# Second attention: scores as two-part float32r products of head pairs in the two row halves of the array, and a full-array bfloat16 matmul ahead of each unit of exponentials

## The chip, the cores and the metric

The kernel runs on one core of one Trainium2 chip. The metric is the device time in microseconds of one execution; three runs of the kernel before stand below. Engines: PE (TensorE matmul), PEld (its weight loads), DVE (VectorE), ACT (ScalarE), POOL (GpSimd), SP (the queue that issues DMAs).

## The reference, cut to what matters

The network is attention A, a two-layer feed-forward stage, attention B, the same feed-forward stage again, each with a residual. Only attention B is changed: 4 sequences of 1024 tokens, 16 heads of 8 dimensions, causal softmax.

```python
Q = split_heads(einsum('bsd,od->bso', x, Wq)); K, V likewise   # x: layer norm of the input
Q = _apply_rope(Q, cos, sin);  K = _apply_rope(K, cos, sin)
logits = jnp.einsum('bhnd,bhmd->bhnm', Q, K) / sqrt(8)
logits = jnp.where(causal, logits, -jnp.inf)
probs = jax.nn.softmax(logits, axis=-1)
attn = jnp.einsum('bhnm,bhmd->bhnd', probs, V)
x = x + einsum('bsd,od->bso', attn, Wo)
```

## The kernel before, in words

Attention B (`attn_b_stage`) works on 16 groups of 4 heads. Queries and keys after the rotation are split into three bfloat16 parts (`first_part`, `second_part`, `third_part`; buffer `RP`, stored to DRAM by `store_parts`). `load(m)` brings a group back so that the nine products of parts times 8 dimensions lie in 72 rows of `QS` and `KS`; three more rows hold the negated row maximum of the scores, so 75 rows are contracted.

Every score is computed twice. A **maximum unit** (`max_unit`, L1661) writes scores of 128 queries against up to 512 keys into one of two one-bank buffers `s1`, on the diagonal after a mask matmul (L1658); DVE reduces the bank to its maximum (L1965). After a group's maxima, POOL splits the 32 negated maxima of each partition into three parts (`offsets`), PE turns them (`turn_unit`, L1670), DVE copies them to `MT` (L1982), and `rows` sends them by one DMA (L1541) into the last three rows of `QS`. An **exponential unit** (`exp_unit`, L1693) writes scores of 128 keys against up to 1024 queries of one head (or several heads of short rows) into one of two two-bank buffers `s2`; ACT writes the exponentials to `PT` (L1876), which holds two key tiles. For groups 3 to 15 POOL zeroes the future part of the diagonal tile (L2089); for groups 0 to 2 a mask matmul (L1688) does it. A **value block** (`value_block`, L1711) multiplies four heads' exponentials with the values, four 128x32 f32 matmuls side by side in the array's columns, into one of two banks `o` (queries 0 to 511, and 512 to 1023); column sums come out with it. ACT copies `o` out (L1865), SP sends it back to rows of heads.

`step(n)` writes the PE order by hand. It runs over 8 slots: in slot j the exponential units of group n for key tile j, the value blocks of tile j-1, and between them the maximum units of group n+1 (slots 0 to 3 of 8) or n+2 (slots 4 to 7), query tiles in the order `MAX_TILES`. A step has 22 exponential units, 12 value blocks of 512, 384, 256 or 128 columns (6, 2, 2, 2 of them), 38 maximum units and 22 mask matmuls. DVE, ACT and POOL follow the same order; each engine works in order, and waits are on counts.

## Time and profile before

| | us |
|---|---|
| median of 3 runs (lowest, highest) | 2239.9 (2236.67, 2242.97) |
| the profiled execution, its own time | 2241.25 |
| its span, first to last instruction | 2239.5 |
| PE busy in the span | 2057.4 (92%) |
| DVE busy | 1786.7 (80%) |
| ACT busy | 1387.7 (62%) |
| POOL busy | 1233.0 (55%) |

The busy shares are averages over stages with different limits. Attention B runs from about 891 us to 1500 us of the span; its first score is written at 928.5 us. The copies of the turned maxima (one in each step) mark the steps. A busy time of PE includes modelled ends of matmuls, so the distance between two starts, not the duration in a row, tells what a matmul cost the array.

### The profile page before, as it was taken

What the parts mean: (1) busy time and instruction counts of PE and PEld (TensorE: products, weight loads), DVE (VectorE), ACT (ScalarE), POOL (GpSimd) and SP (SyncE); (2) the same over time, 40 slices, a digit from 0 to 9 for tenths busy, and PEclk for the clock granted to TensorE, in tenths of its full rate; (3) what the DMA queues carried; (4) which work ended last, traced back from release to release, by engine and by line L of the source; (5) the groups of instructions that cost most, each with busy time, mean ns of one, the idle gap of its engine ahead of it and who ended that gap; (6) DMA issues with size and microseconds to landing.
All of it is one profiled execution on the core that took longest, in us unless ns stands there. A gap on an engine that the chain in (4) does not pass through costs nothing. (4 is left out here: it accounts for less than half of the span.)

```text
span 2239.5 us, 44709 instructions
## 1 busy us (share of the span) xinstructions
PE 2057.4 (92%) x16567; PEld 1066.7 (48%) x16567; DVE 1786.7 (80%) x2386; ACT 1387.7 (62%) x3475; POOL 1233.0 (55%) x633
## 2 busy tenths in 40 slices
PE   5677899999999997899999999968899999999997
PEld 2224555555555553443333333314555555555554
DVE  6986889899999993666777777707899899899993
ACT  8455566666666664446666665665666666766663
POOL 0117777777777771235121222127877777777770
PEclk9799999999999999889999999998999999999999
DMA  2004112112111111303111111122111111111111
GB/s 62 0 3 125 35 34 49 34 36 47 35 43 40 34 34 30 119 29 100 48 44 52 54 40 43 31 61 81 31 44 39 36 43 42 34 44 39 35 34 43
DMA packets 86075, 101.14 MB, mean 45 GB/s; under 512 B 13817, under 2 KB 59841, under 8 KB 83557
## 3 DMA queue, kind: packets, MB, share of 16 engines
q1 hardware_dynamic: 83429, 96.58, 16.8%
q8 instruction: 135, 2.21, 0.4%
q10 hardware_dynamic: 2432, 1.70, 0.3%
q14 instruction: 79, 0.65, 0.1%
HBM read 35.98 MB, written 8.39 MB: 20 GB/s over the span
## 5 line engine op out<-in xcount | busy, mean ns | idle before, releaser
L840 POOL TENSOR_TENSOR ffn_RN<-ffn_SS,ffn_mhalf 128x16 f32<-128x16 f32 x128 | 372.5, 2910 | 272.7 <-DVE ffn_SS L786 272.2
L1965 DVE TENSOR_REDUCE attn_b_NX<-attn_b_s 128x1 f32<-128x512 f32 (+3 forms) x608 | 381.4, 660 | 131.7 <-PE attn_b_s L1661 126.4
L834 POOL TENSOR_TENSOR ffn_QK<-ffn_T 128x1024 f32<-128x1024 f32 x128 | 421.3, 3292 | 20.2 <-DVE ffn_T L734 20.0
L581 ACT ACTIVATE ffn_PB<-ffn_s,ffn_NM 128x128 f32<-128x128 f32 x1024 | 360.6, 391 | 102.6 <-DVE ffn_NM L756 102.6
L1876 ACT ACTIVATE attn_b_PT<-attn_b_s 128x1024 f32<-128x1024 f32 (+3 forms) x352 | 298.1, 870 | 192.3 <-PE attn_b_s L1693 187.9
L625 ACT ACTIVATE ffn_SQ<-ffn_w 128x1024 f32<-128x1024 f32 x128 | 131.1, 1024 | 311.4 <-DVE ffn_T L734 311.1
L828 POOL TENSOR_TENSOR ffn_PB<-ffn_PB,ffn_RDEN 128x1024 f32<-128x1024 f32 x128 | 243.7, 1904 | 27.1 <-DVE ffn_RDEN L719 27.1
L370 PE MATMUL ffn_w<-ffn_Wqkv,ffn_H 128*128 128x512 f32 x512 | 245.9, 603 | 10.5 <-ACT ffn_SQ L625 4.7
L581 ACT ACTIVATION_READ_ACCUMULATOR ffn_PB<-ffn_s,ffn_NM 128x1 f32 x1024 | 236.9, 231 | 0.0
L1661 PE MATMUL attn_b_s<-attn_b_KS,attn_b_QS 72*128 72x512 bf16 (+3 forms) x768 | 220.7, 336 | 6.2 <-DVE attn_b_NX L1965 5.5
L750 DVE TENSOR_TENSOR ffn_QK<-ffn_QK,ffn_RN 128x1024 f32<-128x1024 f32 x128 | 218.7, 1709 | 0.4 <-POOL ffn_RN L840 0.3
L773 DVE COPY ffn_PT<-ffn_w 128x1024 f32<-128x1024 f32 x128 | 156.2, 1221 | 69.3 <-PE ffn_w L424 68.9
L2089 POOL TENSOR_SCALAR_AFFINE_SELECT attn_b_PT<-attn_b_PT 128x512 f32<-128x512 f32 x104 | 66.8, 642 | 252.5 <-ACT attn_b_PT L1876 251.2
L445 PE MATMUL ffn_m<-ffn_HN,ffn_W 128*114 128x512 f32 x360 | 185.9, 613 | 9.0 <-ACT ffn_G L609 3.2
L1693 PE MATMUL attn_b_s<-attn_b_QS,attn_b_KS 75*128 75x512 bf16 (+3 forms) x768 | 187.0, 333 | 5.9 <-ACT attn_b_PT L1876 4.3
L731 DVE TENSOR_TENSOR ffn_T<-ffn_w,ffn_rope 128x1024 f32<-128x1024 f32 x128 | 154.9, 1210 | 40.4 <-PE ffn_w L370 40.2
L1711 PE MATMUL attn_b_o<-attn_b_PT,attn_b_VQ 128*32 128x512 f32 (+3 forms) x1536 | 166.2, 505 | 3.6 <-POOL attn_b_PT L2089 3.3
L756 DVE TENSOR_REDUCE ffn_NM<-ffn_s 128x8 f32<-128x1024 f32 x128 | 155.7, 1217 | 13.5 <-PE ffn_s L412 13.5
L734 DVE TENSOR_TENSOR ffn_T<-ffn_w,ffn_rope 128x512 f32<-128x512 f32 x256 | 163.7, 681 | 0.0
L783 DVE TENSOR_REDUCE ffn_SS<-ffn_SQ 128x16 f32<-128x1024 f32 x128 | 154.6, 1208 | 2.2 <-ACT ffn_SQ L625 2.2
L424 PEld LDWEIGHTS ffn_w<-ident,ffn_PB 128*128 128x128 f32 x1024 | 117.9, 143 | 77.7 <-issue 59.9
L370 PEld LDWEIGHTS ffn_w<-ffn_Wqkv,ffn_H 128*128 128x128 f32 x512 | 95.0, 193 | 119.5 <-issue 82.3
(257 smaller groups left out, 3765.9 us busy)
## 6 DMA issues: line engine op xcount, KB each, us to landing
ffn_Voff<-ffn_Vcur SPq DMA_DIRECT2D x248, 128.0 KB, 2.3
attn_b_QS<-attn_b_qk_parts SPq DMA_DIRECT2D x48, 192.0 KB
attn_b_KS<-attn_b_qk_parts SPq DMA_DIRECT2D x48, 192.0 KB
ffn_H<-ffn_Y SPq DMA_DIRECT2D x64, 128.0 KB, 2.5
ffn_H<-ffn_U SPq DMA_DIRECT2D x64, 128.0 KB, 2.5
attn_b_qk_parts<-attn_b_RP SPq DMA_DIRECT2D x6, 768.0 KB, 4.4
ffn_rope<-in_ffn_rope_dram SPq DMA_DIRECT2D x4, 1024.0 KB, 7.9
attn_b_rope<-attn_b_OS SPq DMA_DIRECT2D x252, 16.0 KB
```

Source lines behind the costliest of these rows:

```text
L370: last = pe.matmul(w0_ps[:, c, :], H1[:, g % 2, b, :], Wqkv[:, l, c, :], start=True, stop=True)
L445: pe.matmul(mlp_bank(g, half, j), W1[:, g // NT, half, j, :], HN[:, :], start=True, stop=True)\
L581: last = act.activation(PB[:, x % 2, e, p, :], s_ps[:, e, p * P:(p + 1) * P], ACT.Exp, bias=NM[:, x % 2, e, p:p + 1], accum_out=DEN[:, x % ...
L750: dve.tensor_tensor(qk, qk, RN[:, x % 2, :].unsqueeze(2).broadcast_to([P, 2 * NH, DH]), ALU.mult)\
L828: pool.tensor_tensor(probs_x, probs_x, by, ALU.mult).then_inc(normed, 1)
L834: pool.tensor_tensor(QK[:, x % 2, :, :, :].rearrange("p c q k -> p (c q k)"), T1[:, :, :, :].rearrange("p c h k -> p (c h k)"), T2[:, :, : ...
L840: pool.tensor_tensor(RN[:, x % 2, :], SS[:, x % 2, :], mhalf[:, :], ALU.pow).then_inc(rnorm, 1)
L1661: last = pe.matmul(bank[:, q * width:(q + 1) * width], QS[0:KS9, m % RING, g + q, i * P:(i + 1) * P], KS[0:KS9, m % RING, g + q, lo:hi], s ...
L1693: last = pe.matmul(bank[:, q * pitch + lo:q * pitch + hi], KS[:, n % RING, g + q, j * P:(j + 1) * P], QS[:, n % RING, g + q, j * P + lo:j ...
L1711: last = pe.matmul(o_ps[half][VCOLS * g:VCOLS * (g + 1), lo - half * 512:512], VQ[:, n % 2, g, j, :], PT[:, j % 2, g, lo - j * P:hi - j * ...
L1876: act.activation(PT[:, j % 2, g:g + pack, 0:width], s2_ps[k % 2][:, 0:pack * pitch].rearrange("p (q w) -> p q w", q=pack)[:, :, 0:width], ...
L1965: dve.tensor_reduce(NX[:, m % 2, c, g:g + pack, i], s1_ps[k % 2][:, 0:pack * (hi - lo)].rearrange("p (q w) -> p q w", q=pack), AX_X, ALU.m ...
```

## The change

All of it is in attention B.

- **Parts.** Rotated queries and keys are split into two float32r parts instead of three bfloat16 ones: one ACT copy (rounded to float32r) and one subtraction for each, instead of two copies and two subtractions. Four products of parts times 8 dimensions take 32 rows.
- **Pairs.** Heads of a group lie in the two halves of the partitions: rows 0 to 63 (`par` 0) and 64 to 127 (`par` 1). Each matmul of scores contracts 62 or 64 rows, some of them zeros (32 terms, zeros, and two rows for the offsets). The zeros and ones are written once by four POOL memsets.
- **Exponential units** hold a pair of heads: 512 queries at most of `par` 0 in one bank of `s2`, of `par` 1 in the other. A step goes over 12 pieces (query half, key tile), with 20 such units. Ahead of the scores of a unit stands a full-array bfloat16 matmul of the identity with the mask table, as many columns as the unit has in a bank, into the bank that the scores then overwrite. In groups 0 to 2 the units on the diagonal have four 64-row mask matmuls instead.
- **Maximum units**: 38 as before, each of one `par`; three banks `s1` instead of two. A mask is two matmuls over 64 rows and 64 columns of keys.
- **Value blocks** stay 12 of the same shapes, but both halves go into one bank `o`; they lag the exponentials by two pieces, and `PT` is a ring of four pieces.
- The offsets take two POOL operations instead of four, the offset rows four DMAs instead of one, a load eight DMAs instead of six.
- `step` spreads the maximum units by columns: behind each exponential unit as many as keep up with the columns of the exponentials.

```diff
-PARTS = 3
-KS9 = PARTS * PARTS * BD
+PARTS = 2
+TERMS = PARTS * PARTS * BD
+NPAR, NPR = 2, 2
+HROWS = P // NPAR
+OFFSETS = HROWS - PARTS
+PIECES_OF = [(0, j) for j in range(4)] + [(1, j) for j in range(8)]
+PRING, PLAG = 4, 2
+S1_BANKS = 3
...
-        s1_ps = [ps(f"s1_{i}", [P, 512]) for i in range(2)]
-        o_ps = [ps(f"o_{i}", [P, 512]) for i in range(2)]
+        s1_ps = [ps(f"s1_{i}", [P, 512]) for i in range(S1_BANKS)]
+        o_ps = ps("o", [P, 512])
...
-                sp.dma_start(QS[KS9:KS9 + PARTS, m % RING, :, :].rearrange("a g t -> a (g t)"), MT[:, m % 2, :])\
-                  .then_inc(s_rows[m % 2], 16)
+                for par in range(NPAR):
+                    for a in range(PARTS):
+                        at = par * HROWS + OFFSETS + a
+                        of = (a * NPAR + par) * NPR * NT
+                        sp.dma_start(QS[at:at + 1, m % RING, :, :].rearrange("a q t -> a (q t)").bitcast(F32),
+                                     MT[of:of + NPR * NT, m % 2, :]).then_inc(s_rows[m % 2], 16)
...
             def max_unit(...):
-                wait(pe, s1_read, k - 1)
+                wait(pe, s1_read, k + 1 - S1_BANKS)
...
-                    last = pe.matmul(bank[:, q * width:(q + 1) * width], QS[0:KS9, m % RING, g + q, i * P:(i + 1) * P],
-                                     KS[0:KS9, m % RING, g + q, lo:hi], start=not diagonal, stop=True,
+                rows = rows_for(par, OFFSETS)
+                for q, (i, c, pr) in enumerate(segments):
+                    last = pe.matmul(bank[:, q * width:(q + 1) * width], QS[rows, m % RING, pr, i * P:(i + 1) * P],
+                                     KS[rows, m % RING, pr, c * 512:c * 512 + width], start=not diagonal, stop=True,
...
+            def exp_unit(n, s, u):
+                bank = [s2_ps[k % 2][:, par * 512:par * 512 + pack * w] for par in range(NPAR)]
+                masked = n < SELECTS and diagonal(s)
+                if masked:
+                    for h in range(2):
+                        for par in range(NPAR):
+                            at = bank[par].rearrange("p (q w) -> p q w", q=pack)[:, :, h * HROWS:(h + 1) * HROWS]
+                            mask(at, par, 1, h, pack, h == 0)
+                else:
+                    pe.matmul(bank[0], keep["identb"][:, :],
+                              causal[:, :, :, :].rearrange("p a b c -> p (a b c)")[:, 0:pack * w], start=True, stop=True,
+                              skip_group_check=True)
                 for q in range(pack):
+                    for par in range(NPAR):
+                        rows = rows_for(par, HROWS)
+                        last = pe.matmul(bank[par][:, q * w:(q + 1) * w],
+                                         KS[rows, n % RING, first + q, j * P:(j + 1) * P],
+                                         QS[rows, n % RING, first + q, lo:hi], start=not masked and q == 0, stop=True,
...
+            def value_block(n, s):
                 if j == 0:
-                    wait(pe, o_read[half], n)
+                    wait(pe, o_read[1 - half], n + half)
...
             def step(n, first):
+                for s in range(NPIECE if 0 <= n < NG else 0):
+                    at = n * NPIECE + s - PLAG
+                    if at >= 0:
+                        value_block(*divmod(at, NPIECE))
+                    for u in range(len(exp_units(s))):
+                        exp_unit(n, s, u)
+                        exps += exp_columns(s, u)
+                        while done < len(scores) and columns * ALL_EXPS < exps * ALL_SCORES:
+                            slot, v = scores[done]
+                            ...
+                                max_unit(m, slot, v)
```

The order on **PE**, in the middle of a step. Before (`s1` maximum units with scores of `KS`, `s2` exponential units, `o` a value block; the last number of a buffer's name is its bank):

```order
L1693 MATMUL attn_b_s2_0<-attn_b_QS,attn_b_KS 128x512
L1693 MATMUL attn_b_s2_0<-attn_b_QS,attn_b_KS 128x384
L1661 MATMUL attn_b_s1_0<-attn_b_KS,attn_b_QS 128x512
L1693 MATMUL attn_b_s2_1<-attn_b_QS,attn_b_KS 128x512
L1693 MATMUL attn_b_s2_1<-attn_b_QS,attn_b_KS 128x384
L1661 MATMUL attn_b_s1_1<-attn_b_KS,attn_b_QS 128x512
L1711 MATMUL attn_b_o_0<-attn_b_PT,attn_b_VQ 32x512 x4
L1661 MATMUL attn_b_s1_0<-attn_b_KS,attn_b_QS 128x512
L1661 MATMUL attn_b_s1_1<-attn_b_KS,attn_b_QS 128x512
L1693 MATMUL attn_b_s2_0<-attn_b_QS,attn_b_KS 128x512
```

PE at the same place of a step, now (L1728 is the added full-array matmul, L1734 the pair of scores for the exponentials, L1677 a mask half, L1696 the scores for a maximum):

```order
L1728 MATMUL attn_b_s2_0<-attn_b_causal,identb 128x512
L1734 MATMUL attn_b_s2_0<-attn_b_QS,attn_b_KS 128x512 x2
L1677 MATMUL attn_b_s1_0<-attn_b_causal 128x64 x2
L1696 MATMUL attn_b_s1_0<-attn_b_KS,attn_b_QS 128x384
L1696 MATMUL attn_b_s1_1<-attn_b_KS,attn_b_QS 128x512
L1728 MATMUL attn_b_s2_1<-attn_b_causal,identb 128x512
L1734 MATMUL attn_b_s2_1<-attn_b_QS,attn_b_KS 128x512 x2
L1696 MATMUL attn_b_s1_2<-attn_b_KS,attn_b_QS 128x512
L1696 MATMUL attn_b_s1_0<-attn_b_KS,attn_b_QS 128x512
L1753 MATMUL attn_b_o<-attn_b_PT,attn_b_VQ 32x512 x4
```

The full-array matmul now stands between 64-row matmuls on either side, and the maximum units come two at a time behind an exponential unit.

The order on **ACT** around the copy of the first query half (`attn_b_OS`) in a step. Before:

```order
L1876 ACTIVATE attn_b_PT<-attn_b_s2_1 128x640
L1876 ACTIVATE attn_b_PT<-attn_b_s2_0 128x2x512
L1876 ACTIVATE attn_b_PT<-attn_b_s2_1 128x2x512
L1876 ACTIVATE attn_b_PT<-attn_b_s2_0 128x2x384
L1865 ACTIVATE attn_b_OS<-attn_b_o_0 128x512
L1876 ACTIVATE attn_b_PT<-attn_b_s2_1 128x2x384
```

ACT there now:

```order
L1925 ACTIVATE attn_b_PT<-attn_b_s2_0 128x1024
L1909 ACTIVATE attn_b_OS<-attn_b_o 128x512
L1925 ACTIVATE attn_b_PT<-attn_b_s2_1 128x1024
L1925 ACTIVATE attn_b_PT<-attn_b_s2_0 128x1024
L1925 ACTIVATE attn_b_PT<-attn_b_s2_1 128x1024
```

The copy reads the bank that the next value block of the other half starts; before, the other half had a bank of its own.

The order on **SP** in one step (results back to rows of heads, offset rows from `MT`, loads of a later group). Before:

```order
L1532 DMA attn_b_rope<-attn_b_OS 8x512 x4
L1536 DMA attn_b_rope<-attn_b_OS 8x512 x4
L1541 DMA attn_b_QS<-attn_b_MT 3x32x128
L1532 DMA attn_b_rope<-attn_b_OS 8x512 x4
L1536 DMA attn_b_rope<-attn_b_OS 8x512 x4
L1514 DMA attn_b_QS<-attn_b_qk_parts 24x1x4096 x3
L1520 DMA attn_b_KS<-attn_b_qk_parts 24x1x4096 x3
```

SP in one step now:

```order
L1553 DMA attn_b_rope<-attn_b_OS 8x512 x4
L1557 DMA attn_b_rope<-attn_b_OS 8x512 x4
L1566 DMA attn_b_QS<-attn_b_MT 1x16x128 x4
L1553 DMA attn_b_rope<-attn_b_OS 8x512 x4
L1557 DMA attn_b_rope<-attn_b_OS 8x512 x4
L1540 DMA attn_b_QS<-attn_b_qk_parts 16x1x2048 x4
L1540 DMA attn_b_KS<-attn_b_qk_parts 16x1x2048 x4
```

The places are the same; the offset rows are four DMAs in a row, the load eight.

## Rows read from the trace of the kernel before

**Rows 1.** Busy time by stretch: us, engines busy (count), PE clock, DMA share, GB/s

```profile
972.90:1008.60 35.70, 34.77 (x199) 13.44 (x199) 24.64 (x42) 18.27 (x22) 8.28 (x8) 0.76 0.01 2
...
1363.40:1394.80 31.40, 30.04 (x217) 10.83 (x215) 24.11 (x42) 19.49 (x26) 6.46 (x13) 1.00 0.17 48
...
1457.70:1488.60 30.90, 25.30 (x186) 6.65 (x184) 0.27 (x1) 23.04 (x30) 7.23 (x12) 0.94 0.07 14
```

**Rows 2.** Instructions on tile `attn_b_s`: duration ns min/median/max, first and last start us

```profile
L1982 DVE CAST attn_b_MT<-attn_b_s x16: 274/276/288, 972.9 to 1457.7; 96x128 bf16<-96x128 f32 x16
```

**Rows 3.** Waits in 1363.4 to 1394.8 us: us in total, times, longest us

```profile
ACT attn_b_PT L1876 <- PE attn_b_s L1693: 12.6, 14, 1.6
PEld attn_b_s L1658 <- DVE attn_b_NX L1965: 7.7, 15, 0.8
DVE attn_b_NX L1965 <- PE attn_b_s L1661: 7.0, 13, 0.8
```

**Rows 4.** Timeline of PE inside steps: start us, duration us, instructions

```profile
1249.81 0.38 PE L1661 MATMUL attn_b_s<-attn_b_KS,attn_b_QS 72*128 72x512 bf16 x1
1250.12 1.06 PE L1711 MATMUL attn_b_o<-attn_b_PT,attn_b_VQ 128*32 128x512 f32 x8
1251.11 0.23 PE L1658 MATMUL attn_b_s<-attn_b_causal,identb 128*128 128x128 bf16 x1
...
1251.40 0.22 PE L1658 MATMUL attn_b_s<-attn_b_causal,identb 128*128 128x128 bf16 x1
1251.46 0.38 PE L1661 MATMUL attn_b_s<-attn_b_KS,attn_b_QS 72*128 72x512 bf16 x1
1251.68 0.49 PE L1693 MATMUL attn_b_s<-attn_b_QS,attn_b_KS 75*128 75x512 bf16 x2
...
1372.23 0.43 PE L1711 MATMUL attn_b_o<-attn_b_PT,attn_b_VQ 128*32 128x128 f32 x8
1372.59 0.39 PE L1658 MATMUL attn_b_s<-attn_b_causal,identb 128*128 128x512 bf16 x1
```

**Rows 5.** Timeline of PE in the second feed-forward stage, at its 64x64 tiles

```profile
1703.57 0.59 PE L379 MATMUL ffn_w<-ffn_Wqkv,ffn_H 128*128 128x512 f32 x1
1704.09 0.41 PE L403 MATMUL ffn_s<-ffn_masks,identb 64*64 64x512 bf16 x4
1704.33 1.04 PE L412 MATMUL ffn_s<-ffn_KT,ffn_QT 64*64 64x128 f32 x32
1705.30 1.11 PE L445 MATMUL ffn_m<-ffn_HN,ffn_W 128*114 128x512 f32 x2
```

**Rows 6.** Groups by form, 1363.4 to 1394.8 us: busy us, mean ns | idle before, releasers

```profile
L1965 DVE TENSOR_REDUCE attn_b_NX<-attn_b_s 128x1 f32<-128x512 f32 x24 | 15.6, 687 | 3.1 <-PE attn_b_s L1661 3.0
...
L1876 ACT ACTIVATE attn_b_PT<-attn_b_s 128x1024 f32<-128x1024 f32 x7 | 6.8, 1027 | 4.3 <-PE attn_b_s L1693 4.3
...
L1865 ACT ACTIVATE attn_b_OS<-attn_b_o 128x512 f32<-128x512 f32 x3 | 1.8, 592 | 0.0
```

**Rows 7.** Busy time by stretch (columns as in rows 1), at the lower clock

```profile
976.40:983.10 6.70, 6.70 (x23) 2.92 (x23) 3.53 (x6) 3.56 (x4) 1.16 (x1) 0.50 0.01 2
...
928.50:938.70 10.20, 9.15 (x39) 7.58 (x40) 2.67 (x4) 3.08 (x4) 4.36 (x3) 0.50 0.48 151
```

**Rows 8.** The offset rows of the first group, and what PE does next (timeline)

```profile
973.24 0.81 SPq L1541 DMA_DIRECT2D attn_b_QS<-attn_b_MT  x1
...
977.35 1.06 PE L1693 MATMUL attn_b_s<-attn_b_QS,attn_b_KS 75*128 75x512 bf16 x2
```

**Rows 9.** The third parts on DVE (timeline), and a memset on POOL (group by form)

```profile
912.45 2.43 DVE L1942 TENSOR_TENSOR attn_b_RP<-attn_b_TA,attn_b_RP 128x1024 bf16<-128x1024 f32 x2
...
L2024 POOL MEMSET attn_b_VQ<- 128x2048 f32 x1 | 1.8, 1804 | 0.0
```

**Rows 10.** Last step, without maximum units: its first scores and last copy (timeline)

```profile
1462.19 1.04 PE L1693 MATMUL attn_b_s<-attn_b_QS,attn_b_KS 75*128 75x512 bf16 x4
...
1487.94 0.60 ACT L1865 ACTIVATE attn_b_OS<-attn_b_o 128x512 f32<-128x512 f32 x1 [1.33 <-PE attn_b_o L1711]
```

More of the change, by code:

```diff
@@ new lines, in turn_unit @@
+                pe.wait_ge(parts, PARTS * (m + 1))
+                pe.matmul(s1_ps[k % S1_BANKS][0:PARTS * BG * NT, 0:P],
+                          NP[:, m % 2, :, :, :, :].rearrange("p a g h i -> p (a g h i)").bitcast(F32),
+                          keep["ident"][:, :], start=True, stop=True).then_inc(s1_mm, 1)
+            def exp_unit(n, s, u):
+                k = s2_at[n, s, u]
+                half, j = PIECES_OF[s]
+                first, pack = exp_units(s)[u]
+                lo, hi = piece(s)
+                w = hi - lo
@@ L1690, in exp_unit @@
-                for q in range(pack):
-                    for lo in range(0, width, 512):
-                        hi = min(width, lo + 512)
-                        last = pe.matmul(bank[:, q * pitch + lo:q * pitch + hi],
-                                         KS[:, n % RING, g + q, j * P:(j + 1) * P],
-                                         QS[:, n % RING, g + q, j * P + lo:j * P + hi],
-                                         start=(q * pitch + lo) % 512 == 0 if selected else lo > 0, stop=True,
+                if (s, u) == (0, 0):
+                    pe.wait_ge(s_rows[n % 2], 16 * ROWS * (n // 2 + 1))
@@ new lines, in begin_maxima, with score_columns, exp_columns @@
+            def begin_maxima(m, slot, u):
+                if u == 0 and slot == MAX_SPLIT:
+                    if m == 0:
+                        pe.wait_ge(s_set, SETS)
+                    pe.wait_ge(s_load[m % RING], 16 * LOADS * (m // RING + 1))
+            def score_columns(slot, u):
+                return max_units(slot)[u][1] * len(max_units(slot)[u][2])
+            def exp_columns(s, u):
+                return NPAR * width(s) * exp_units(s)[u][1]
+            ALL_SCORES = sum(score_columns(slot, u) for slot in range(NT) for u in range(len(max_units(slot))))
@@ L1951, in _ @@
             remainder(1)
-            for w in range(2):
-                third_part(w)
             for c in range(4, NCH):
```

489 lines of the change are left out of this document (241 added, 248 removed).

## The prediction

> **What bounds the kernel now.** I read the busy times by stretch first, then the waits of one undisturbed step, then PE's timeline inside it. Only attention B changes, so only its steps count. The copies of the turned maxima are one step apart: the first starts at 972.9, the sixteenth at 1457.7 us [rows 2], so 15 steps take 484.8 us; the step at 1363.4 is 31.4 us long with a full clock, and the first step 35.7 us with a clock of 0.76 [rows 1]. In the undisturbed step DVE is busy for 24.1 us, ACT for 19.5 [rows 1]: neither is full. PE's 30.0 us contain modelled ends, so I count its stream from start to start instead.
>
> 512 columns of bfloat16 scores take 0.22 us (1251.46 to 1251.68), 128 columns of a mask 0.06 (1251.40 to 1251.46), a value block of 512 columns 0.99 with the way out of it (1250.12 to 1251.11), one of 128 columns 0.36 (1372.23 to 1372.59), and the way into one 0.31 - 0.22 = 0.09 (1249.81 to 1250.12) [rows 4]. A group has 4 heads x 36 tiles x 128 = 18432 columns of scores, 36 times 512, and computes them twice. The stream of a step: scores 2 x 36 x 0.22 = 15.8; masks 32 x 0.06 = 1.9; value blocks 6 x 0.99 + 2 x 0.78 + 2 x 0.57 + 2 x 0.36 = 9.4 (the middle widths between the two read); ways in 12 x 0.09 = 1.1. Sum 28.2. The remaining 3.2 us of 31.4 are waits: PE's weight loads wait for DVE to free one of two banks, DVE waits 7.0 us for PE, ACT 12.6 [rows 3]. So PE bounds the step, and DVE stands 4 us behind it.
>
> **The change, part by part.** All per step of a group unless said.
>
> Value blocks keep shape and number: 9.4 + 1.1 = 10.5.
>
> Scores for the exponentials: 18 pairs of 512 columns. If two matmuls in different row halves run together, a pair costs 0.22: 18 x 0.22 = 4.0, instead of 7.9. What speaks for it: in the feed-forward stage 64x64 tiles in two row and two column halves take 32 records of 128 columns in 0.97 us (1704.33 to 1705.30); one f32 record of 512 full-array columns takes 0.52 - 0.09 = 0.43, so 32 records of 128 one after another would take 3.4 [rows 5]. Four tiles do run together. No row shows two tiles of 64 rows and 128 columns; bounds 4.0 and 7.9, I take 4.0.
>
> The type float32r is in no row. Bounds: bfloat16's 0.22 for 512 columns [rows 4], and f32, where one matmul of the program is two records of 0.43 [rows 5]. I take 0.22: the operands are rounded when they are written and split into two parts again, so they carry fewer bits than the f32 numbers that need the second record and the double passes.
> The Trainium skill (FP8 and Floating Point Precision, TensorE Precision Notes) says that true FP32 makes four passes and that a reduced-precision FP32 operand is truncated to FP22, the array's own width; by it the cost is one pass too, and no trace here shows it.
>
> Scores for the maxima with masks: 38 units as before. Alone they cost 36 x 0.22 = 7.9 and 44 mask halves x 0.06 = 2.6, in all 10.5; all in pairs half of that, 5.3. Going along PE's new order and letting only neighbours of different halves run together I count 6.3. Before: 7.9 + 1.9 = 9.8.
>
> The added full-array matmuls: as many columns as the pairs, 18 x 0.22 = 4.0. They stand between 64-row matmuls. A change of tile shape costs: 64x64 tiles follow a full-array matmul 0.52 instead of 0.43 us after its start (1703.57 to 1704.09) [rows 5], value blocks cost the 0.09 above. There are 20 such matmuls, 40 changes; 12 of the ways in come from a value block, whose way out is counted, and the turned maxima add two: 30 x 0.09 = 2.7. Bounds 0 (if full and 64-row, 128-column matmuls share a mode) and 30 x 0.14 = 4.2.
> The Trainium skill (TensorEngine Tiling, Key Properties) states that changing the tiling mode drains TensorE, which speaks against this change: by it all 30 changes cost, without it the sum would be 2.7 lower; rows 5 agree with it for the shapes they show.
>
> New stream: 10.5 + 4.0 + 6.3 + 4.0 + 2.7 + 0.3 (turn in f32) = 27.8, against 28.2. The pairs' gain of 7.4 is nearly spent on the added matmuls and their changes of shape.
>
> Waits, 3.2 before. A third bank for maxima: DVE still needs 0.69 for 512 columns [rows 6] and gets units two at a time; for a full-width piece (PE 2.65, DVE 4 x 0.69 = 2.76) I laid the units out and got 2.96, because the fourth unit must wait for a bank. Bounds: nothing, and all 3.2; I take -1.5. The single bank `o`: at two places PE's next half must wait for ACT's exponential (1.03) and the copy behind it (0.59) [rows 6], 1.8 us after the scores, while PE has 1.2 to 1.5 us of work there: 0.3 to 0.7 each, +1.0 in all; queued behind this wait are the next exponential unit and the maxima, so DVE waits too. Offset rows: one DMA issue takes 0.81 us, and PE used the rows 4.1 us after that issue began [rows 8]; three more issues make it up to 6.5, while from the turn to the step's end there are about 7. Together with weight loads of four-byte numbers, which come in twos behind each change of shape, +0.6 (bounds 0 and 3). So a step takes 27.8 + 3.2 - 1.5 + 1.0 + 0.6 = 31.1, i.e. -0.3; 15 steps -4.5.
>
> The last step has no maxima: its first scores start at 1462.2, its last copy at 1487.9 [rows 10], 26 us, bound by the chain exponential, select, value block, two pieces deep. With four pieces ACT's 20 us of exponentials and copies should bound it, or PE's 10.5 + 4.0 + 4.0 + 3.0 = 21.5, about 23: -3 (bounds -5 and 0). Start: DVE loses 2.4 us of third parts [rows 9], partly waited for elsewhere; value products now wait for ACT's copy of the single bank. -1.5 (bounds -4 and +3). The four memsets of 6144 columns take 3 times the 1.8 us of 2048 [rows 9] each, 22 us, beside the layer norm, in which POOL has nothing to do: nothing. Eight loads instead of six lie in SP's slack.
>
> Sum: 2241.25 - 4.5 - 3 - 1.5 = 2232.2 on the profiled execution's own time, which lies 1.35 above the median: 2231.
>
> **The rivals.**
> 1. *DVE becomes the bound.* PE's changes of shape fall into waits or cost less, the third bank feeds DVE without gaps. DVE's 24.1 us and a tenth for gaps and the wait at `o` make 28.5: 15 x -2.9 - 4.5: about 2192. For it: waits were equal on both sides before. Against it: PE's stream alone is 27.8.
> 2. *The row halves do not run together* (the other sign). Where: at each pair, since the second matmul's weights arrive late or the tiles exclude each other. Then scores cost 4.0 more and maxima 4.2 more, a stream of 36.0, with 1.5 of waits 37.5: 15 x 6.1 - 1.5, about 2329. If only the maxima run alone, 34.5: 2284. It decides early: my whole gain is 9 us, 0.6 a step, so with 36 pairs in a step (18 for the exponentials, 18 for the maxima) a loss of 0.02 us in each, a tenth of the 0.22, turns the sign. For it: one row above shows only 64-column tiles.
> 3. *The clock.* From 976.4 to 983.1 us PE was busy all the time with scores of 72 and 75 rows and the clock stayed at 0.50; from 928.5 it rose only after f32 value products of 128 rows [rows 7]. So it matters how much of the array works. The added full-array matmuls and the pairs speak for 2.4 GHz; lone 64-row matmuls and masks, and waits, speak against it. At 1.2 GHz the 24 us of columns double: 52 a step. All of the stage: about 2540; a third of it: about 2340.
> 4. *float32r takes more passes.* Two: +4.0 and +5, a step of 38, about 2340. Four: above 2600.
>
> **How the numbers follow.** The forecast (PE's stream swapped for one of equal length, 2205 to 2255) has 0.52, rival 1 0.18 (2180 to 2205), rival 2 0.13, rival 3 0.10, rival 4 0.07. A measurement of this kernel tells 0.3% (6.7 us) from no change. Faster than 2233.2: half of the forecast's case and rival 1, 0.45; within 0.3%: 0.16; slower: the rest of the forecast's case and rivals 2 to 4, 0.39. Both signs have weight, so the likeliest case's own range is 2205 to 2255; the range that should hold 8 times in 10 reaches from 2185, inside rival 1, to 2340, past rival 2 and the mild forms of 3 and 4.
>
> **What would show it.** Distance of the turned maxima: 31.1 here, 28.5 for rival 1, 34 and more for the others. Starts of a pair of L1734 within some ns, then 0.22 to the next: right. L1728 to L1734 0.31: the change of shape costs. Waits of L1753 for ACT's L1909 near 1 us a step. DVE near 24 us busy in 31. Clock 1.00 from the fourth step on. If the first scores of a step wait for DMA of the offset rows, my 0.6 was too small.

## The result: 1.6% slower, and the profile after

The changed kernel takes 2275.05 us (median of 4 runs, 2274.68 to 2276.26) against 2238.45 us for the kernel before (4 runs beside them): a ratio of 1.016, interval 1.0148 to 1.0172. The forecast was 2231. The profiled execution's span is 2273.1 us, 33.6 more than before. A step is the work on one group, from one copy of the turned maxima to the next; the time that a matmul holds PE is the distance from its start to the start of what follows.

The copies of the turned maxima divide these 33.6 us. First the tile's group of instructions, which answers to [rows 2], then busy times by stretch (us, engines busy (count), granted clock of PE, DMA share, GB/s), which answer to [rows 1]: first step, a late step, last step.

```profile
L2020 DVE COPY attn_b_MT<-attn_b_s x16: 273/273/282, 982.9 to 1489.1; 64x128 f32<-64x128 f32 x16
```

```profile
982.88:1013.06 30.18, 28.97 (x225) 15.48 (x226) 23.21 (x42) 17.58 (x19) 7.23 (x6) 0.83 0.01 2
...
1386.59:1420.67 34.08, 32.35 (x255) 14.88 (x258) 23.35 (x41) 19.50 (x22) 5.92 (x12) 1.00 0.17 41
1489.10:1527.70 38.60, 29.77 (x216) 10.19 (x218) 0.28 (x1) 23.35 (x29) 7.62 (x12) 0.98 0.08 14
```

- The first copy comes at 982.9 instead of 972.9 us: +9.9.
- The first three steps take 94.3 instead of 104.0 us: -9.7. The first was 35.7 us at a clock of 0.76 before [rows 1] and is 30.2 at 0.83; the third was 36.2 at 0.91 and is 32.0 at 1.00. So a good part of this gain is the granted clock and not the change.
- The other twelve take 411.9 instead of 380.7: +31.2. An ordinary one is 34.1 us where it was 31.4 [rows 1], both at a clock of 1.00; the seventh and the eleventh, which also hold the output products of a sequence, are 1.9 longer in both kernels.
- From the last copy to the end: +2.2. The last step takes 38.6 us, where before the next stage began 34.6 us after the copy: +4.0. What follows, which is not changed, was 1.8 shorter (745.4 instead of 747.2).

The profiled execution took 2274.8 us by its own time, 42.6 more than the 2232.2 forecast for it: 26.0 in the fifteen steps (+21.5 instead of -4.5), 11.4 at the start, 7.0 in the last step, less the 1.8.

The matmuls inside such a step, PE's timeline (start us, duration us, instructions), to be held against [rows 4]:

```profile
1290.58 0.39 PE L1728 MATMUL attn_b_s<-attn_b_causal,identb 128*128 128x512 bf16 x1
1290.90 0.50 PE L1734 MATMUL attn_b_s<-attn_b_QS,attn_b_KS 64*128 64x512 f32 x2
1291.24 0.40 PE L1696 MATMUL attn_b_s<-attn_b_KS,attn_b_QS 62*128 62x512 f32 x2
1291.57 0.39 PE L1728 MATMUL attn_b_s<-attn_b_causal,identb 128*128 128x512 bf16 x1
```

Two matmuls of 64 rows stand in one row (x2): the row halves run together, and 512 columns of float32r take hardly longer than 512 of bfloat16 (0.24 us from start to start in the lines below, where the forecast had 0.22), so float32r makes one pass. L1728 holds PE 0.32 us, 0.22 of columns and 0.10 of change of shape. But the pair behind it holds PE 0.34 us, not 0.22; its record is 0.50 long, that of the maxima's pair behind it 0.40. The same pairs in the run of experiment 7, which has no added matmul (L1730 is L1734 there, and the maxima are still L1696):

```profile
1330.52 0.50 PE L1730 MATMUL attn_b_s<-attn_b_QS,attn_b_KS 64*128 64x512 f32 x2
1330.85 0.40 PE L1696 MATMUL attn_b_s<-attn_b_KS,attn_b_QS 62*128 62x512 f32 x2
1331.09 0.40 PE L1730 MATMUL attn_b_s<-attn_b_QS,attn_b_KS 64*128 64x512 f32 x2
1331.33 0.93 PE L1696 MATMUL attn_b_s<-attn_b_KS,attn_b_QS 62*128 62x512 f32 x2
```

At 1330.52 the pair comes right behind a value block: 0.33 to the next. At 1331.09 it comes behind other 64-row matmuls: 0.24. So about 0.1 us hangs on what stands ahead. The weight loads (engine, count, ns min/median/max) suggest on what:

```profile
L1734 PEld LDWEIGHTS attn_b_s<-attn_b_QS,attn_b_KS x48: 182/183/186, 1388.0 to 1418.6; 64*128 64x128 f32 x48
L1696 PEld LDWEIGHTS attn_b_s<-attn_b_KS,attn_b_QS x48: 182/187/188, 1388.3 to 1420.4; 62*128 62x128 f32 x48
...
L1728 PEld LDWEIGHTS attn_b_s<-attn_b_causal,identb x20: 95/96/96, 1387.7 to 1418.3; 128*128 128x128 bf16 x20
```

The record of a load of four-byte weights is twice as long as that of one of bfloat16. The Trainium skill (TensorE: Matmul & The Clock Gate, Weight-path perf modes) says that the fast weight load works with 128 weights and types other than FP32, about twice as fast; 95 against 183 to 188 ns agree.

**Theory A**: the pair behind a change of shape shows its weight load, 0.12 us in each of 20 units, 2.4 us a step, and this is what the forecast lacked. **Theory B**: the single output bank and maxima that find no bank free make the excess. **Theory C**: the clock.

### The profile page after: what moved, and what is told of

It is laid out like the page before. It is cut to its first block and busy times, and to the rows that moved or that the text cites. A ratio compares the mean times of both kernels' runs of the same rounds, so it can differ in the third digit from the quotient of the medians.

```text
span 2273.1 us, 46087 instructions
## 1 busy us (share of the span) xinstructions
PE 2090.5 (92%) x17225; PEld 1128.5 (50%) x17282; DVE 1771.9 (78%) x2383; ACT 1380.7 (61%) x3435; POOL 1234.9 (54%) x599
## 5 line engine op out<-in xcount | busy, mean ns | idle before, releaser
L2007 DVE TENSOR_REDUCE attn_b_NX<-attn_b_s 128x1 f32<-128x512 f32 (+3 forms) x608 | 370.4, 657 | 175.3 <-PE attn_b_s L1696 171.3
L1925 ACT ACTIVATE attn_b_PT<-attn_b_s 128x1024 f32<-128x1024 f32 (+1 forms) x320 | 298.0, 939 | 222.2 <-PE attn_b_s L1734 216.5
L633 ACT ACTIVATE ffn_SQ<-ffn_w 128x1024 f32<-128x1024 f32 x128 | 131.1, 1024 | 311.5 <-DVE ffn_T L742 311.2
L1696 PE MATMUL attn_b_s<-attn_b_KS,attn_b_QS 62*128 62x512 f32 (+3 forms) x768 | 191.8, 400 | 0.3 <-DVE attn_b_NX L2007 0.3
L1753 PE MATMUL attn_b_o<-attn_b_PT,attn_b_VQ 128*32 128x512 f32 (+3 forms) x1536 | 164.5, 500 | 7.9 <-issue 4.8
L1734 PE MATMUL attn_b_s<-attn_b_QS,attn_b_KS 64*128 64x512 f32 (+3 forms) x768 | 156.4, 428 | 14.4 <-issue 9.6
```

The source lines that it names most:

```text
L1696: last = pe.matmul(bank[:, q * width:(q + 1) * width], QS[rows, m % RING, pr, i * P:(i + 1) * P], KS[rows, m % RING, pr, c * 512:c * 512 + ...
L1753: last = pe.matmul(o_ps[VCOLS * g:VCOLS * (g + 1), lo - half * 512:512], VQ[:, n % 2, g, j, :], PT[:, (n * NPIECE + s) % PRING, g, 0:hi - ...
L1925: act.activation(out, bank, ACT.Exp).then_inc(probs, 1)
L2007: dve.tensor_reduce(at, bank, AX_X, ALU.max, negate=True).then_inc(s1_read, 1)
```

## The experiments

The table shows ordinary steps at a clock of 1.00, for the runs that tell where the time goes. PE's stream by line is added up from the single records, from start to next start, over one step (for the kernel after four of the twenty records of L1728 are missing; its 5.9 goes by the twenty records of the half-reduction run, and what then stands too high at their neighbours is taken off):

```
                               step   value   added   exp    max+mask+turn
                                      blocks  matmul  pairs  with waits     median us
forecast                       31.1    9.4     5.8    4.0    11.9           2231
kernel after                   34.1    9.4     5.9    6.5    12.2           2275.1
no added matmul                30.2    9.4     -      6.1    14.7           2234.1
half the reduction             32.6    9.4     6.0    6.5    10.7           2253.6
both                           28.0    9.4     -      5.7    12.9           2191.8
two output banks               37.8    9.4     6.0    7.7    14.6           2342.9
```

(The forecast's row puts each 0.09 of change with the matmul ahead of it, and all 3.3 of its waits in the last column.)

**1 to 4. The added matmul**: taken out, made of two row halves, short, doubled.

```
-                else:
-                    pe.matmul(bank[0], keep["identb"][:, :], causal[...][:, 0:pack * w], start=True, ...)
```

> The kernel after without the added full-array matmul in each unit of exponentials; nothing else is changed and the outputs are the same. Theory A (the added matmul costs its columns, the change of tile shape and a weight load that nothing hides behind it: 0.22 + 0.10 + 0.12 = 0.44 us for each of 20 units, 8.8 a step): a step falls from 34.1 to 25.3 on PE; DVE's 23.4 us busy with a tenth for gaps holds it at about 26, and the whole at 2275 - 16 x 8 = about 2150, if the granted clock stays at 1.00. Theory B (the excess over the forecast comes from the single output bank and from maxima that are not paired): the added matmul costs 6.7, a step 27.4, the whole about 2168. Theory C (it is this matmul that keeps the clock at 1.00): the clock falls to 0.50 in the steps, a step is 38 to 45 us, the whole 2340 to 2450.

Measured: 2234.14 us, ratio to before 0.998 (0.9968 to 0.9992); an ordinary step 30.2 us. Two steps of this run:

```profile
1136.00:1171.38 35.38, 33.81 (x239) 15.76 (x238) 23.02 (x42) 21.28 (x26) 5.92 (x11) 0.81 0.16 39
1329.33:1359.54 30.21, 28.14 (x239) 13.44 (x238) 22.98 (x42) 18.87 (x22) 5.92 (x11) 1.00 0.19 46
```

The added matmul costs 3.9 us a step, not the 8.8 that A gave it nor the 6.7 of B, and the kernel without it is 0.2% faster than the kernel before: so the numbers of A and B are wrong. Where it is gone, the maxima and what they wait for hold PE 2.5 us longer (table): it stood partly where PE would have waited. It would not have waited for DVE alone. With half of DVE's reduction gone (experiments 6 and 7) this column grows by 2.2 us all the same, and without the added matmul (experiment 7) one step shows waits for DVE and for ACT's copy of the output bank (us in total, times, longest):

```profile
PEld attn_b_s L1696 <- DVE attn_b_NX L2004: 1.4, 3, 0.5
...
PE attn_b_o L1749 <- ACT attn_b_OS L1905: 0.7, 1, 0.7
```

Of C something may be true: in this execution four steps behind the first run at 0.81 to 0.95 of the clock, which together adds some 11 us; in the kernel after they all show 1.00. Experiment 12 has none of these matmuls and shows 1.00, too, so that they hold the clock up isn't shown.

```
-                    pe.matmul(bank[0], keep["identb"][:, :], causal[...][:, 0:pack * w], ...)
+                    for par in range(NPAR):
+                        rows = rows_for(par, HROWS)
+                        pe.matmul(bank[par], keep["identb"][rows, :], causal[rows, ...][:, 0:pack * w], ...)
```

> The added full-array matmul is replaced by two of 64 rows, one in each row half and bank of the pair, of the same number of columns: the tile shape of the scores, so nothing changes shape between them and the weight loads have something to hide behind. The whole array still works. Theory A: of the 0.44 us a unit only the 0.22 of columns stay, a step is 34.1 - 20 x 0.22 = 29.7, the whole about 2205, clock 1.00. Theory B: the change of shape costs 0.09 alone, a step is 34.1 - 2 = 32.1, the whole about 2243. Theory C: the clock stays at 1.00, as in the kernel after.

Measured: 2236.14 us (0.9978; 0.9963 to 0.9993), a step 31.4 us: 2.7 under the kernel after, nearer to B's 32.1 than to A's 29.7. The same columns without a change of shape cost 1.2 us a step, and all steps but the first show a clock of 1.00. PE's timeline says why they are cheap:

```profile
1410.35 0.39 PE L1730 MATMUL attn_b_s<-attn_b_causal,identb 64*128 64x512 bf16 x2
1410.38 0.58 PE L1736 MATMUL attn_b_s<-attn_b_QS,attn_b_KS 64*128 64x512 f32 x2
1410.81 0.23 PE L1677 MATMUL attn_b_s<-attn_b_causal 64*128 64x64 bf16 x4
```

1024 columns in each row half take 0.46 us, 0.43 of columns and 0.03 more; the pair alone took 0.33 behind a value block. The added columns lie partly beside the pair's weight load.

The third keeps only the first 64 columns (`bank[0][:, 0:64]`), the fourth writes the matmul twice.

> The added full-array matmul is kept, but has 64 columns instead of up to 512: its columns are taken away, its changes of shape and the weight loads behind them stay. Theory A: 0.44 - 0.19 = 0.25 us a unit stay, a step is 34.1 - 18 x 0.19 = 30.7, the whole about 2221 if the clock holds. Theory B: 0.12 a unit stay, a step 29.5, the whole about 2200. Theory C: with few full-array columns the clock falls, the whole is over 2300.

Measured: 2245.21 us (1.0026; 1.0005 to 1.0047), a step 32.0. So of the 3.9 us, 1.8 are changes of shape with the loads behind them and the 64 columns that stay, 2.1 are the other columns. Neither A's 30.7 nor B's 29.5 was reached, since both started from too large a cost of the whole matmul. The clock is 1.00 in all steps but the first.

> The added full-array matmul stands twice in each unit. Theory A: the second has the shape and the weights of the first and costs its columns alone, 18 x 0.22 = 3.9 us a step: a step 38.0, the whole 2275 + 16 x 3.9 = about 2337. Theory B: PE is not what a step waits for all the time, and part of the 3.9 falls into waits: the whole 2300 to 2320. Theory C: no gain from more full-array work, since the clock is at 1.00 already, except in the first step, whose 0.83 would rise: 2 us less.

Measured: 2310.97 us (1.0324; 1.0296 to 1.0352), a step 36.9: +2.8, as B had it (its 3.9 in part hidden).

**5. The banks of the kernel before**, two for the outputs and two for the maxima (`S1_BANKS = 2`, `o_ps` two banks, each half with its own).

> The kernel after with its banks dealt out as in the kernel before: two output banks, two banks for the maxima. Theory A (in the kernel after PE's own stream fills the step; its waits are small): the wait for ACT's copy of the output bank goes (0.7 to 1.0 us a step), PE waits more for DVE to free one of two banks; a step between 33.5 and 35, the whole 2268 to 2290. Theory B (the single output bank is what made the step longer than the forecast): a step of 32 or less, the whole under 2250.

Measured: 2342.91 us (1.0469; 1.0438 to 1.05). Theory B falls in its first half, and A's size was wrong, too: with two banks for the outputs and two for the maxima a step is 3.7 us longer.

```profile
1330.63:1368.38 37.75, 36.64 (x259) 15.62 (x259) 24.19 (x40) 21.59 (x26) 5.93 (x11) 1.00 0.16 37
```

The table shows where: +2.4 at the maxima, +1.2 behind exponential pairs, whose next maxima wait for a bank. PE "busy" at 36.6 contains these waits.

**6 and 7. DVE's share.** Both let DVE reduce the first half of the columns only (`bank[..., 0:width // 2]`), with and without the added matmul.

> The kernel after, except that DVE takes each maximum over the first half of its columns alone (the offsets are not the true maxima then); PE's work is the same. It takes about 7 us of DVE's 23.4 out of a step. Theory A (PE's stream sets the step of the kernel after): a step stays at 33 to 34. Theory B (PE and DVE take turns in being late, over three banks): the step falls to 31 or less, near the forecast.

> The same, without the added full-array matmuls. Theory A (without them DVE is late in the pieces with wide maxima, PE in those with wide value blocks, and a step costs the longer of the two piece by piece): a step falls from 30.2 to about 26 or 27, PE's own stream. Theory B (PE's stream is 30 even without the added matmuls, so that they hide somewhere else): it stays at 29 to 30.

```profile
1369.80:1402.36 32.56, 32.08 (x261) 14.32 (x259) 14.39 (x41) 19.50 (x23) 5.92 (x11) 1.00 0.17 43
```

```profile
1323.49:1351.49 28.00, 27.15 (x241) 13.17 (x239) 14.01 (x40) 18.86 (x23) 5.92 (x11) 1.00 0.21 49
```

With DVE's work cut from 23.4 to 14.4 us a step falls by 1.5 us with the added matmul (2253.6 us, one run) and by 2.2 without (2191.8, one run). Neither number was forecast: 32.6 lies between A's 33 to 34 and B's 31, 28.0 between A's 26 to 27 and B's 29 to 30. So PE's stream, with its waits for ACT, makes most of the step of the kernel after, and waiting for DVE 1.5 us of it. In the records of L1696, 7 of a step's starts lie within 0.02 us of the one before in the kernel after, 13 with half the reduction: in the kernel after a second maximum of a pair often finds its bank still being read.

**8. Is it the weight load?** Between the full-array matmul and the pair stand two more of 64 rows and up to 256 columns.

```
+                    for par in range(NPAR):
+                        rows = rows_for(par, HROWS)
+                        pe.matmul(bank[par][:, 0:min(256, w)], keep["identb"][rows, :], causal[rows, ...], ...)
```

> The kernel after with two more matmuls of 64 rows, one in each row half and up to 256 columns wide, between the full-array matmul and the pair of scores. Theory A (behind a change of shape the pair pays 0.12 us for its weights of four-byte numbers, which nothing hides): the new columns lie beside that load and cost next to nothing, at most 0.04 us a unit, 0.8 a step; a step of 34.1 to 34.9, the whole 2275 to 2288. Theory B (the 0.12 us is part of the change of shape itself): 20 x 0.11 = 2.1 us more a step, 36.2, the whole about 2309.

Measured: 2274.56 us (2 runs), a step 34.3 us: +0.25 for 2.0 us of columns. The step lies in A's range, far from B's 36.2.

```profile
1414.14 0.39 PE L1728 MATMUL attn_b_s<-attn_b_causal,identb 128*128 128x512 bf16 x1
1414.46 0.28 PE L1733 MATMUL attn_b_s<-attn_b_causal,identb 64*128 64x256 bf16 x2
1414.50 0.48 PE L1739 MATMUL attn_b_s<-attn_b_QS,attn_b_KS 64*128 64x512 f32 x2
1414.82 0.53 PE L1696 MATMUL attn_b_s<-attn_b_KS,attn_b_QS 62*128 62x512 f32 x2
```

From the change of shape (1414.46) to the next matmul behind the pair it is 0.36 us instead of 0.34, with 256 columns (0.11 us) more in each row half. A cost of the change itself would have come on top of them. So the 0.12 us are time of the pair that other columns of its shape can cover, as its weight load is: theory A, as far as the pairs go. The kernel before agrees. There scores with bfloat16 weights pay next to nothing behind a value block: two matmuls of 384 columns hold PE 0.34 us, 0.32 of them by their columns.

```profile
1456.09 1.07 PE L1711 MATMUL attn_b_o<-attn_b_PT,attn_b_VQ 128*32 128x512 f32 x8
1457.09 0.50 PE L1693 MATMUL attn_b_s<-attn_b_QS,attn_b_KS 75*128 75x384 bf16 x2
1457.43 0.22 PE L1670 MATMUL attn_b_s<-identb,attn_b_NP 128*96 128x128 bf16 x1
```

That it is the load itself, and not another time of a four-byte pair that can be covered, is inferred: no run has pairs with other weights in the new shape.

**9. Without the masks of the maxima** (`diagonal = False`).

> The kernel after without the masks of the maxima (the maxima are then taken over keys of the future too; the exponentials are still masked or selected). It takes 44 bfloat16 matmuls of 64 rows out of a step. Theory A (a mask costs 0.03 to 0.04 us itself, and the four-byte weight load of the scores behind it lies open for 0.12): PE's stream falls by 1.4 + some 16 x 0.1 = 3.0 us, of which DVE gives back a part: a step of 31.5 to 32.5. Theory B (only the masks' own time): a step of 32.7 to 33.5.

Measured: a step of 32.5, -1.55 (2241.7 us, one run), at the border between A and B. The records say more: the 44 masks held PE for 1.4 us of the step of the kernel after, and the maxima hold it for 10.0 in both runs (missing records of L1728 taken off). So nearly all of the gain is the masks' own time, B's cause, and no weight load behind a mask came free. The whole time isn't to be compared: this execution had a clock of 1.00 at the start of the stage, and its first copy came at 974.2 instead of 982.9 us.

**10 and 11. The start of the stage.** Ahead of each unit of the first group's maxima stands one more full-array matmul, as wide as the unit, then of 64 columns; the second form also in the kernel of experiment 12.

> The kernel after with one more full-array bfloat16 matmul ahead of each unit of the first group's maxima, which stand between the products of the stage's start. Theory A (the first 55 us are longer because the clock stays at 0.50 from 928 to 952.5 us): the clock rises there by 940, the first copy of the turned maxima comes at 971 to 975 instead of 982.9 us, the whole is 8 to 10 us shorter, about 2266. Theory B (the start is longer because the value products wait for ACT's copy of the one output bank): the clock may rise, but the first copy stays at 981 to 983.

> The kernel after with one more full-array bfloat16 matmul of 64 columns (up to 512 in the earlier run of this kind) ahead of each unit of the first group's maxima. Theory A (the clock makes the 10 us of the start): it is at 1.00 from about 930 on, the first turn comes at 972 to 977 us, the whole is 6 to 10 us shorter, 2265 to 2269. Theory B (PE's stream makes them, through more changes of shape between products and maxima): the first turn stays at 981 or later, and the whole at 2274 or above.

> The same in the kernel without added matmuls in the units of exponentials and with the maxima spread evenly (2222.0 us). Theory A: 6 to 10 us less, 2212 to 2216. Theory B: 2222 or above. Where the steps have no added matmul, a fall of the clock in single steps can hide 5 us of either.

The kernel after from 928 to 952 us, and the same two stretches in the run with the doubled matmul, whose code up to the first turn is the same:

```profile
928.00:940.00 12.00, 11.30 (x52) 8.70 (x53) 4.65 (x8) 3.59 (x5) 5.38 (x3) 0.53 0.52 134
940.00:952.00 12.00, 12.00 (x36) 5.61 (x36) 5.02 (x8) 1.62 (x2) 2.34 (x1) 0.50 0.68 233
```

```profile
928.00:940.00 12.00, 10.99 (x75) 7.07 (x75) 7.66 (x14) 5.32 (x7) 4.87 (x3) 1.00 0.49 129
940.00:952.00 12.00, 11.42 (x47) 5.16 (x46) 7.17 (x12) 2.30 (x4) 7.22 (x4) 1.00 0.72 241
...
L2023 DVE COPY attn_b_MT<-attn_b_s x16: 272/273/282, 971.5 to 1514.7; 64x128 f32<-64x128 f32 x16
```

One code, two clocks: 982.9 at 0.50, 971.5 at 1.00. Part of the 11.4 us lies ahead of the stretch: PE's first mask starts at 928.55 in the one and at 926.98 in the other. From there to the first copy it is 54.3 and 44.6 us, so the clock makes 9.8 us of the start. Nine profiled executions have this code up to the first turn. Seven have a mean clock of 0.50 to 0.58 from 928 to 952 us and take 52.8 to 57.8 us; two, the one above and that of experiment 13, have 1.00 and take 44.6. The kernel before takes 44.5, with 10.2 of them at 0.50. But to buy the clock is as dear: with wide matmuls the clock is 0.72 and 1.00 in these stretches, the first copy comes at 987.3, and the whole takes 2286.47 us (1.0219; 1.0181 to 1.0258); with short ones 0.86 and 1.00, 980.4, 2275.56 us, no change. The third kernel takes 2215.48 us (0.9889) against 2221.96 without, which lies in A's range; but the intervals overlap, and the first copy came only 2.8 us earlier. A is right on the cause of the time; the cure gives nothing that is clear of noise.

**12 to 14. Can both kernels be beaten?** First the kernel of experiment 1 with the maxima spread by the columns of the value blocks, too; then the same with a 64-column full-array matmul behind each value block; then with the maxima that fall due by a value block ahead of it.

```
                     if at >= 0:
                         value_block(*divmod(at, NPIECE))
+                    exps += value_columns(s)      # 4 heads x width; ALL_EXPS grows alike
```

> The kernel without the added matmuls (first experiment), in which the order on PE spreads the maxima by the columns of the value blocks too, four columns for one, and not by those of the exponentials alone. Theory A (a step is the sum, piece by piece, of the later one of PE and DVE, since three banks carry DVE only some 2 us): DVE is fed in the pieces with wide value blocks, too; a step falls from 30.2 to 27 to 28.5, near the 28.0 of the run with half the reduction, the whole to 2190 to 2210 if the clock holds as before. Theory B (the 2 us that DVE adds come from the order inside a piece): the step stays at 30.

Measured: 2221.96 us (0.9908; 0.9881 to 0.9935). A step is 29.7, as B had it to within 0.3, and A's size failed; more of the gain is the clock, which showed 1.00 in every step but the first of the profiled execution. DVE still stood still once, here in DVE's timeline, and PE's beside it:

```profile
1237.35 1.29 DVE L2008 TENSOR_REDUCE attn_b_NX<-attn_b_s 128x1 f32<-128x512 f32 x2 [1.69 <-PE attn_b_s L1696]
```

```profile
1235.58 1.06 PE L1749 MATMUL attn_b_o<-attn_b_PT,attn_b_VQ 128*32 128x512 f32 x8 [0.80 <-ACT attn_b_OS L1910]
1236.58 0.50 PE L1730 MATMUL attn_b_s<-attn_b_QS,attn_b_KS 64*128 64x256 f32 x4
1236.92 0.63 PE L1696 MATMUL attn_b_s<-attn_b_KS,attn_b_QS 62*128 62x512 f32 x3
```

PE waits for the copy of the one output bank, then works on a value block of 1 us, then on exponentials, and only then makes a maximum: DVE waits 1.69 us.

> The same order with a full-array matmul of 64 columns in the first unit of each piece of exponentials alone, right behind a value block. Theory A (behind a value block the change of shape is paid anyhow, 0.52 us to the scores; and short matmuls are enough for the clock, since with 64 columns in every unit all steps took 32.0 us at a clock of 1.00): 12 x 0.03 to 0.1 us more than in the run without them, a step 0.4 to 1 us longer, but none of the steps of 31.7 to 35.4 us with a clock under 1.00, which cost 11 us in all; the whole within 5 us of the even spread alone, or under it. Theory B (each short matmul costs a full change of shape): a step 2 us longer.

Measured: 2225.52 us (0.9935; 0.9916 to 0.9954), a step 30.9, +1.2: more than A's 0.4 to 1, while the whole lies within A's 5 us. All ordinary steps have the full clock, but here there was nothing left to gain by it.

> The kernel with the maxima spread evenly, in which those that are due by the columns of a value block stand ahead of that block on PE, not behind the exponentials that follow it. Theory A (DVE starves because maxima are queued behind PE's wait for the output bank and behind the 1 us of a value block): the step falls from 29.7 to 27.5 to 28.8, the whole to 2190 to 2210. Theory B (PE now waits for DVE ahead of the block, and the exponentials are late instead): a step of 29.5 or more, the whole 2220 or above.

```
+                    for u in range(-1, len(exp_units(s))):
+                        if u == 0 and at >= 0:
                             value_block(*divmod(at, NPIECE))
+                        if u >= 0:
                             exp_unit(n, s, u)
+                        exps += exp_columns(s, u) if u >= 0 else value_columns(s)
```

Measured: 2209.33 us (2203.56 to 2215.57), ratio 0.9863 (0.9833 to 0.9893): the lowest median of the kernels that compute all of the maxima, 1.4% under the kernel before. Its interval overlaps those of the even spread with and without short matmuls at the start (2215.48 and 2221.96), so its lead over them isn't shown. A step is 29.35, only 0.35 less, and A's 27.5 to 28.8 was not reached, while the time lies inside its range: the steps with output products became 31.6 instead of 32.5, the one after the first turn 27.7 (clock 0.88) instead of 30.0 (clock 0.83), and the part behind the last turn takes 780.7 us instead of 786.8.

```profile
1338.79:1368.13 29.34, 27.40 (x246) 13.37 (x238) 23.05 (x42) 18.67 (x22) 5.92 (x11) 1.00 0.20 47
```

## Why the prediction was wrong

It named a small gain, 9 us, and 33.6 were lost in the profiled execution. The step that failed is the price of a pair of scores for the exponentials: 0.22 us, with all loads of four-byte weights at 0.6 us a step. The runs show 0.34 us behind a change of shape, 2.5 us a step. It is the largest part of the miss, next to a start that the forecast had at -1.5 us and that came out at +9.9, nearly all of it by the clock. Point by point, in its order:

- **Value blocks 10.5** with their ways in: the 9.4 are right in every run of the table, the ways in at 12 x 0.09 aren't. From the last maximum of 512 columns to the block it is 0.41 to 0.43 us, where it was 0.31 [rows 4]:

```profile
1367.11 0.48 PE L1696 MATMUL attn_b_s<-attn_b_KS,attn_b_QS 62*128 62x512 f32 x1
1367.51 0.85 PE L1753 MATMUL attn_b_o<-attn_b_PT,attn_b_VQ 128*32 128x384 f32 x8
```

  The twelve ways in, with the maximum ahead of each, take 4.4 us in a step of the kernel after; the forecast's sizes give 3.0. In the table this 1.4 lies in the last column. Why they are dearer isn't told apart by any run, but for 0.3 us of it (below).
- **Pairs at 0.22**: they do run together, in one pass. This is the step that failed, by its size. The forecast took 0.22 for each of 18 from bfloat16 rows [rows 4] and put all loads of four-byte weights, with the offset rows, at 0.6 us (bounds 0 and 3). Measured are 6.5 us instead of 4.0 for the pairs: 20 units with 0.12 us of open weight load each (0.34 us for 512 columns, 0.28 for 384). This is 2.5 of the 3.0 us by which a step is longer than forecast. Rows at hand spoke for it only faintly: PE's loads of the kernel before were bfloat16 or stood in value blocks, and the one f32 change in [rows 5] has no 64-row, 128-column tile.
- **Added matmuls 4.0 and changes 2.7**: the matmul and the change behind it are right, 0.32 us at 512 columns. That they could be taken out for 6.7 would have been wrong: 3.9, since PE then waits more.
- **Maxima with masks 6.3, and waits of 3.3**: the sum was right by luck. In the table the last column has 12.2 where the forecast had 11.9 with changes and waits. With half of DVE's work gone 10.7 stay, of which 2.3 were forecast as changes and turn: 8.4 instead of 6.3, as the ways into value blocks are dearer, fewer pairs form, PE waits for the output bank, and narrow maxima follow each other at 0.11 us where columns ask for 0.05. The waits that DVE makes are 1.5 by experiment 6, where the forecast had 3.3 of waits in all.
- **Third bank -1.5, single output bank +1.0**: together -0.5 forecast, -3.7 measured against the reverse trade. The sign that the prediction named, waits of L1753 for L1909 near 1 us a step, did not come. At one of the two places PE waits for the copy of the output bank:

```profile
1364.65 0.40 PE L1696 MATMUL attn_b_s<-attn_b_KS,attn_b_QS 62*128 62x512 f32 x1
1365.37 1.07 PE L1753 MATMUL attn_b_o<-attn_b_PT,attn_b_VQ 128*32 128x512 f32 x8 [0.33 <-issue]
```

  The copy ends at 1365.27, and it is 0.72 us between these starts where it is 0.42 with two output banks (experiment 5); at the other place both have 0.35. So the single bank costs 0.3 us a step here, and by that the third bank for the maxima is worth about 4, an estimate from the 3.7.
- **Last step -3**: +4.0. PE's timeline of the last step shows PE as the bound, piece after piece (ACT stands idle for 0.57 us in each of these pieces, waiting for L1734):

```profile
1511.85 0.39 PE L1728 MATMUL attn_b_s<-attn_b_causal,identb 128*128 128x512 bf16 x1
1512.16 0.50 PE L1734 MATMUL attn_b_s<-attn_b_QS,attn_b_KS 64*128 64x512 f32 x2
1512.60 0.39 PE L1728 MATMUL attn_b_s<-attn_b_causal,identb 128*128 128x512 bf16 x1
1512.92 0.49 PE L1734 MATMUL attn_b_s<-attn_b_QS,attn_b_KS 64*128 64x512 f32 x2
1513.34 1.06 PE L1753 MATMUL attn_b_o<-attn_b_PT,attn_b_VQ 128*32 128x512 f32 x8
1514.34 0.39 PE L1728 MATMUL attn_b_s<-attn_b_causal,identb 128*128 128x512 bf16 x1
```

  2.49 us a piece where ACT needs 2 x 1.02. By the forecast's own sizes it is 0.99 + 0.09 + 4 x 0.22 + 3 x 0.09 = 2.23; the difference is the two open loads. The first scores and the last copy, which answer to [rows 10] (timeline, then the copies' group):

```profile
1495.89 0.50 PE L1734 MATMUL attn_b_s<-attn_b_QS,attn_b_KS 64*128 64x512 f32 x2
```

```profile
L1909 ACT ACTIVATE attn_b_OS<-attn_b_o x32: 590/592/597, 1001.2 to 1523.4; 128x512 f32<-128x512 f32 x32
```

  Between them lie 27.5 us, 25.8 in [rows 10]; 2.3 more lie between the turn and those scores. The forecast took PE's sum and ACT's sum for it and left out the end, where each piece is again a chain of exponential, select and value block.
- **Offset rows**: four transfers instead of one, and in fifteen of the sixteen groups PE didn't wait for them, in the first for 0.3 us; so what the prediction had at +0.6 together with the weight loads is all weight loads.
- **Start -1.5**: +9.9. The stretch was named in rival 3 and its rows were read [rows 7]: at a clock of 0.50 until f32 products of 128 rows came. The clock stayed low until 952 instead of 938.7 us, though such products ran before (eight records of L1634 from 938.54 on, at 0.50), and two executions of the same code had 1.00. So the rival's reading, that it matters how much of the array works, isn't borne out; what holds the clock down there is open. The rival priced the steps and forgot the start.
- **Of the rivals** none came. 1 (DVE) is what is left when the added matmul and half of the reduction go: 28.0 a step, 2191.8 us (one run), as priced (28.5, 2192), though DVE is busy for only 14.0 us there and it is PE's stream with its waits that is 28.0. 2 and 4 are excluded by the timeline; in 2, the 34.5 for maxima alone is no sum of its own terms, which give 27.8 + 4.2 + 1.5 = 33.5 and about 2270. 3 decided the start and part of the first three steps. The place of the sign was in the sentence of rival 2: with 36 pairs, 0.02 us each turn it; 0.12 came in 20 of them.

## What to carry to other kernels

A matmul's price is its columns only if something of the same shape stands ahead for its weights to load behind; take a pair with four-byte weights behind a change of shape as 0.1 us dearer, as it was here, and put cheap work of the same shape there if some must be added at all. Work that is added where the engine waits in between costs less than its own length (3.9 of 6.0 us here), and a clock that changes over a stage has to be priced at its start as well. With a few banks between two engines, their number and the order in which the feeder takes up its other work count (3.7 and 0.9 us of a step here): the kernel with the lowest time here differs from the changed one in no operation but those 20 matmuls that are left out, and in where the maxima stand.

## What the runs showed of the hardware that I had not expected

- 256 columns of bfloat16 in each row half, behind a change of shape and ahead of float32r scores, cost 0.01 to 0.03 us (0.25 a step for 20 units) where the columns alone are 0.11.
- A full-array matmul of 64 columns in each unit, 20 in a step of 32 us, went with a clock of 1.00 in all steps but the first, none at all with 0.81 to 0.95 in four more of them; yet another kernel without any (the evenly spread one) had 1.00 in all but the first. What lets it fall is open.
- The same code ran from 928 to 952 us at a mean clock of 0.50 to 0.58 in seven executions and at 1.00 in two. Between first mask and first copy this is 44.6 us or some ten more.
- The Trainium skill (TensorE: Matmul & The Clock Gate, LDWEIGHTS) gives a load of 128 columns as 128/1.2 = 107 ns whatever the rows; the open 0.10 to 0.12 us fit, the records of 182 to 188 ns don't.
